# Turning the normed rows of the FFN stage by a round trip through memory and one VectorE instruction, in place of TensorE's transposes

## What is computed

```python
x   = x + tanh(g_xattn[0]) * xattn(_layernorm(x), ctx)          # stages 1 and 2
u   = _layernorm(x)                                             # stage 3 from here
mu  = mean(u); var = mean(square(u - mu))
h   = (u - mu) * rsqrt(var + EPS) * ln_gamma + ln_beta          # 4096 x 512
y   = silu(h @ w1 + fc1_bias)                                   # 4096 x 2048
z   = y @ w2 + fc2_bias                                         # 4096 x 512
out = x + tanh(g_ffn[0]) * (u + 0.5 * z)
```

## Time and profile before

| | us |
|---|---|
| median of 3 runs (1665.62 to 1668.49) | 1667.76 |
| the profiled execution | 1669.8 |
| its span in the trace | 1668.0 |
| PE busy in the span | 1631.2 |
| DVE busy | 848.6 |
| ACT busy | 569.1 |
| POOL busy | 366.3 |

### The profile page before, as it was taken

How to read it: one execution, slowest core, us unless ns; L and a number is a source line. 1 busy time by engine, 2 the same in 40 slices (tenths; PEclk the granted TensorE clock), 3 DMA queues, 4 the chain that set the end, 5 groups by cost and what they waited for, 6 DMA issues and landing times.

```text
span 1668.0 us, 20697 instructions
## 1 busy us (share of the span) xinstructions
PE 1631.2 (98%) x7746; PEld 1341.2 (80%) x7746; DVE 848.6 (51%) x1732; ACT 569.1 (34%) x990; POOL 366.3 (22%) x562
## 2 busy tenths in 40 slices
PE   8999999999999999899999899999999999999999
PEld 6887888877788887687877688888888888888887
DVE  6757454486764444688888955232333232333311
ACT  5432121234222112575666433232223222322322
POOL 1212100022111000488888801000000000000000
PEclk9999999999999999899999999999999999999999
DMA  6302110131221105454554432101010101010000
GB/s 210 107 21 95 44 51 26 49 109 52 70 76 39 38 26 170 133 164 152 164 165 158 132 109 74 40 1 51 1 51 1 51 1 51 1 51 1 26 1 26
DMA packets 66760, 116.19 MB, mean 70 GB/s; under 512 B 11185, under 2 KB 11185, under 8 KB 66507
## 3 DMA queue, kind: packets, MB, share of 16 engines
q1 hardware_dynamic: 64864, 111.41, 20.7%
q10 hardware_dynamic: 1797, 3.46, 0.6%
HBM read 80.00 MB, written 34.84 MB: 69 GB/s over the span
## 4 chain that ended last, share of the span: by engine, by line
PE 91%; DVE 4%; POOL 2%; issue 1%; DMA 1%; ACT 1%; DVEq 0%; SPq 0%; ACTq 0%; POOLq 0%
PE banks L719 86%; PE banks L729 3%; PE banks L929 2%; DVE split L1662 1%; DMA tile_x<-x_scratch 1%; DMA plain<-in_L_xattn_Wk 0%; POOL split L1537 0%; DVE plain L1793 0%; DVE split_q L1662 0%; DVE plain L2025 0%; POOL split L1544 0%; POOL small L1525 0%; ACT plain L1246 0%; DVE plain L2203 0%; DVE plain L2208 0%
## 5 line engine op out<-in xcount | busy, mean ns | idle before, releaser
L719 PE MATMUL banks<-split_q,split 128*128 128x512 f32 x2328 | 571.4, 395 | 4.9 <-POOL split L1537 3.2
L719 PE MATMUL banks<-split 128*128 128x512 f32 (+5 forms) x2304 | 543.4, 385 | 8.4 <-DVE split L1662 5.8
L719 PEld LDWEIGHTS banks<-split_q,split 128*128 128x128 f32 x2328 | 431.3, 188 | 96.2 <-POOL split L1537 4.1
L719 PEld LDWEIGHTS banks<-split 128*128 128x128 f32 (+3 forms) x2304 | 412.7, 185 | 106.7 <-DVE plain L1793 7.1
L719 PE MATMUL banks<-split,split_q 128*128 128x512 f32 (+3 forms) x1728 | 391.7, 379 | 7.2 <-DVE split_q L1662 4.3
L719 PEld LDWEIGHTS banks<-split,split_q 128*128 128x128 f32 x1728 | 308.3, 189 | 58.0 <-DVE split_q L1662 5.1
L1662 DVE TENSOR_TENSOR split<-banks,split 128x512 fp32r<-128x512 f32 (+5 forms) x232 | 146.3, 638 | 153.0 <-ACT split L1119 152.2
L2168 DVE TENSOR_TENSOR split<-plain,split 128x512 fp32r<-128x512 f32 x128 | 88.5, 692 | 257.8 <-ACT split L1438 257.8
L1119 ACT ACTIVATE split<-banks 128x512 fp32r<-128x512 f32 (+5 forms) x232 | 124.3, 557 | 247.2 <-PE banks L929 191.1
L1432 ACT ACTIVATE plain<-banks,small 128x512 f32<-128x512 f32 x128 | 88.0, 688 | 289.2 <-PE banks L719 289.2
L1662 DVE TENSOR_TENSOR split_q<-banks,split_q 128x512 fp32r<-128x512 f32 x68 | 46.7, 687 | 220.2 <-ACT split_q L1119 220.0
(11 more groups left out here) (155 smaller groups left out, 1259.2 us busy)
## 6 DMA issues: line engine op xcount, KB each, us to landing
plain<-in_x SPq DMA_DIRECT2D x64, 256.0 KB, 2.7
xo_scratch<-plain SPq DMA_DIRECT2D x32, 256.0 KB, 2.3
x_scratch<-plain SPq DMA_DIRECT2D x32, 256.0 KB, 2.0
plain<-x_scratch SPq DMA_DIRECT2D x32, 256.0 KB, 3.0
tile_x<-xo_scratch SPq DMA_DIRECT2D x32, 256.0 KB, 3.1
xg_scratch<-tile_x SPq DMA_DIRECT2D x32, 256.0 KB, 2.0
out<-plain SPq DMA_DIRECT2D x32, 256.0 KB, 2.1
tile_x<-x_scratch SPq DMA_DIRECT2D x28, 256.0 KB, 5.0
```

What stands on the lines that cost most here:

```text
L719: mm = nc.tensor.matmul(out, left(c, l), right(c, r), start=start and c == 0 and (l, r) == PASSES[0], stop=stop and c == chunks - 1 and (l ...
```

## The change

The next tile's normed block is no longer transposed by PE. SP stores the 128x512 block from `H0[:, 0]` to a scratch tensor in DRAM and reads it back with four loads into `HB` (the other half of `H0`). Load i fills partitions 32i to 32i+31; in them, each partition takes 16 runs of 32 floats (128 bytes). After that, the four loads together have placed every 32x32 square where its transpose belongs, but not yet turned in itself. One DVE instruction (`nc.vector.transpose`) turns all squares of the block in place, from `HB` into PSUM bank 2 or 3. `hi_h` and `lo_h` read the bank as before. Scaling and shifting are done one pass earlier (`NORM_AT = (6, 8, 10, 12)`), as are `base_x`, the statistics and the addition of `bias3`. `TURN_AT` is unchanged. `h_scale` waits for the store of the block before it, since the store reads the single buffer.

```diff
+NORM_AT = (6, 8, 10, 12)
 TURN_AT = (7, 9, 11, 13)
+QB = P // 32
...
+        h_dram = nc.dram_tensor("h_scratch", (TILE, E), F32, kind="Internal").ap()
...
+        HB = H0[:, 1]
...
+            def store_h(t, k):
+                sp.wait_ge(hn_ready, t * BT + k + 1)
+                if t > 1:
+                    sp.wait_ge(tp_full, (t - 1) * BT + TP3 + k + 1)
+                sp.dma_start(h_dram[k * P:(k + 1) * P, :], H0[:, 0]).then_inc(h_out, 16)
+            def load_hb(t, k):
+                sp.wait_ge(h_out, ((t - 1) * BT + k + 1) * 16)
+                sp.wait_ge(tp_full, t * BT + TP3 + k)
+                rows = h_dram[k * P:(k + 1) * P, :].rearrange("(q s) (c i r) -> i s c q r", q=QB, c=C, i=QB)
+                for i in range(QB):
+                    sp.dma_start(HB[32 * i:32 * i + 32].rearrange("p (c q r) -> p c q r", c=C, q=QB),
+                                 rows[i]).then_inc(hb_in, 16)
             for f in range(4, NF):
...
+                if f >= 8 and f % 2 == 0:
+                    store_h(1, f // 2 - 4)
+                    load_hb(1, f // 2 - 4)
...
             for t in range(NT):
+                if 0 < t < NT - 1:
+                    for k in range(BT):
+                        store_h(t + 1, k)
+                        load_hb(t + 1, k)
                 store_out(t, t % 2)
...
 # PE, tile3
                     ffn_out(t, f)
-                    if f in TURN_AT and not last:
-                        turn_h(t + 1, TURN_AT.index(f))
...
 # ACT, tile3
                     if f in TURN_AT and not last:
                         hi_h(t + 1, 1 - slot, TURN_AT.index(f))
-                    if f + 1 in TURN_AT and not last:
-                        k = TURN_AT.index(f + 1)
+                    if f + 1 in NORM_AT and not last:
+                        k = NORM_AT.index(f + 1)
                         base_x(t + 1, 1 - slot, k, base[:, 1 - slot, k])
...
 # DVE
             def h_scale(t, k, x):
-                dve.wait_ge(tp_full, t * BT + TP3 + max(k - 1, 0))
+                if t == 0:
+                    dve.wait_ge(tp_full, TP3 + max(k - 1, 0))
+                else:
+                    dve.wait_ge(tp_full, TP3 + BT)
+                    if (t - 1) * BT + k:
+                        dve.wait_ge(h_out, ((t - 1) * BT + k) * 16)
...
+            def turn_h(t, k):
+                dve.wait_ge(hb_in, ((t - 1) * BT + k + 1) * QB * 16)
+                nc.vector.transpose(PS[:, 2 + k % 2], HB).then_inc(tp_full, 1)
...
 # DVE, tile3, behind lo_hid3 (and, in tile 0, lo_w and scale_w2)
-                        if f + 2 in TURN_AT:
-                            k = TURN_AT.index(f + 2)
+                        if f + 2 in NORM_AT:
+                            k = NORM_AT.index(f + 2)
...
-                        if f + 1 in TURN_AT:
-                            h_shift(t + 1, TURN_AT.index(f + 1))
-                        if f - 1 in TURN_AT:
-                            k = TURN_AT.index(f - 1)
+                        if f + 1 in NORM_AT:
+                            h_shift(t + 1, NORM_AT.index(f + 1))
+                        if f in TURN_AT:
+                            turn_h(t + 1, TURN_AT.index(f))
+                        if f - 1 in NORM_AT:
+                            k = NORM_AT.index(f - 1)
...
-                        if f == TURN_AT[0] - 3:
+                        if f == NORM_AT[0] - 3:
                             stats_x3(p3, base[:, 1 - slot], (b_in[1 - slot], (t + 1) // 2 * 16 + 16 * (1 - slot)))
                         if f in TURN_AT:
                             lo_h(t + 1, 1 - slot, TURN_AT.index(f))
```

More of the change, by code:

```diff
@@ L428, in build @@
         o_out = [sem("o_out_0"), sem("o_out_1")]
+        h_out, hb_in = sem("h_out"), sem("hb_in")
         block = ctx.enter_context(nc.Block())
@@ L2200, in h_scale @@
             def h_scale(t, k, x):
-                dve.wait_ge(tp_full, t * BT + TP3 + max(k - 1, 0))
-                nc.vector.scalar_tensor_tensor(out=H0[:, k % 2], in0=x, scalar=mvX[:, k, 0:1], in1=vec3[:, 0],
+                if t == 0:
[4 more added lines that the diff above has]
+                        dve.wait_ge(h_out, ((t - 1) * BT + k) * 16)
+                nc.vector.scalar_tensor_tensor(out=H0[:, 0 if t else k % 2], in0=x, scalar=mvX[:, k, 0:1], in1=vec3[:, 0],
                                                op0=ALU.subtract, op1=ALU.mult).then_inc(x3_scaled, 1)
@@ L2207, in h_shift @@
                 dve.wait_ge(x3_scaled, t * BT + k + 1)
-                nc.vector.scalar_tensor_tensor(out=H0[:, k % 2], in0=H0[:, k % 2], scalar=rsH[:, k:k + 1],
+                h = H0[:, 0 if t else k % 2]
+                nc.vector.scalar_tensor_tensor(out=h, in0=h, scalar=rsH[:, k:k + 1],
                                                in1=vec3[:, 1], op0=ALU.mult, op1=ALU.add).then_inc(hn_ready, 1)
             def lo_h(t, slot, k):
-                lo_t(TP3 + k, [hT[:, slot * C:(slot + 1) * C, h, k * P:(k + 1) * P] for h in range(2)],
-                     k, t, BT)
+                halves = [hT[:, slot * C:(slot + 1) * C, h, k * P:(k + 1) * P] for h in range(2)]
+                lo(TP3 + k, halves[1], quarters(PS[:, 2 + k % 2]), halves[0], t, BT)
+            def turn_h(t, k):
+                dve.wait_ge(hb_in, ((t - 1) * BT + k + 1) * QB * 16)
+                nc.vector.transpose(PS[:, 2 + k % 2], HB).then_inc(tp_full, 1)
             kept = None
```

## The result

| | before | after |
|---|---|---|
| median, us | 1667.47 (4 runs) | 1653.12 (4 runs, 1652.21 to 1656.21) |
| profiled execution, us | 1669.8 | 1656.2 |
| its span, us | 1668.0 | 1654.4 |

The ratio is 0.9911, 95% interval 0.9897 to 0.9925. The kernel is 14.4 us faster; 19.2 were forecast. The direction and the range held, but 4.8 us are missing. The two traces say where.

A forecast was written before the change was run, and what follows sets the result against it. PE was taken as the bound, busy all of stage 3; removing 28 turns of 0.684 us saves 19.2 us, everything added being hidden at cost 0, so 1667.76 becomes 1648.6 us; range 1645.5 to 1660.

The forecast's parts named there:

- A turn costs 0.684 us of PE: Stage 3, PE: each of 28 turns, transposes plus the wait behind them, costs 0.684 us; removing all saves 19.2 us.
- DVE's transpose at 0.69 us: DVE, one added transpose per block: 0.69 us, ends 0.5 and 3.0, hidden behind PE's matmuls at cost 0.
- The round trip in steady tiles hidden: SP and DMA, tiles 1 to 6: store lands after 2.0 us, gather 3.3 us before DVE asks; cost 0.
- the bounds: DMA engines: a 128-byte packet takes near 0.018 us, with ends of 0.012 and 0.103 us.
- The cover of 3.4 us: DVE's transpose in a turn pass: it may come 3.4 us later than +3.94 and still cost PE nothing.
- Earlier statistics in tile 0: Tile 0, DVE: statistics moved earlier wait 1.1 us for the load of tile 1's rows, inside 2.94 us slack.
- SP's queue in tile 0: Tile 0: w2's loads queue behind `load_hb` by some 1 to 2 us; cost 0, up to 4 us kept for range.
- the next pass makes it up: Tile 0, DVE's turn passes: work plus wait exceeds 5.44 by 1.9 us, inside 2.94, and is recovered one pass later.
- rival B: Transposes go but a wait of the present size stays each turn, giving back 9.2 us: 1657.9; chance 0.09.
- Rival A: DVE's wait on `hb_in`: gather loads land too late, 65 us lost at the upper end, 1733 us; chance 0.08.
- Rival C: Gather loads split into 4-byte pieces, 4096 packets per engine, 1120 us more, near 2770; chance 0.02.
- the 100 of the estimate: Gather loads: by the Trainium skill's rule on plain DMAs that transpose by strides, a block would take some 100 us.

The follow-up runs named there:

- serial_4s: Changed kernel; in tiles 1 to 6 each gather load waits for the one before, and the block is stored three times in sequence: 1714.45 us, ratio 1.0274.
- serial_4: Changed kernel; in tiles 1 to 6 each gather load is issued when the one before has landed: 1653.14 us, ratio 0.991.
- no_trip_0: Changed kernel without tile 0's block stores and gather loads, so DVE turns what the buffer holds: 1648.03 us, ratio 0.9875.
- w2_and_base_first: Changed kernel with w2's odd load ahead of the gather and the load of tile 1's rows one pass earlier: 1649.42 us, ratio 0.9886.

## Why the prediction was right, and which term was wrong

- **A turn costs 0.684 us of PE** and all of it goes: right. Tiles 1 to 6 went from 89.78 to 87.04 us. The split of that cost was off: transposes 0.48 and wait 0.20, not 0.56 and 0.12. The sum did not hang on it, since both went.
- **DVE's transpose at 0.69 us**: 0.72 measured, inside the ends of 0.5 and 3.0.
- **The round trip in steady tiles hidden**: right, with the store landing after 2.0 us as taken. Each load's issue took 0.63 us, not 0.44. The packets cost less. The first window goes from a store to behind its gather, the other two split it into store and gather (columns as in the earlier trace rows):

```profile
1071.50:1080.00 8.50, 8.50 (x39) 7.05 (x38) 1.58 (x3) 1.46 (x3) 0.00 (x0) 1.00 0.28 62
...
1071.75:1073.80 2.05, 2.05 (x11) 1.70 (x10) 0.00 (x0) 0.00 (x0) 0.00 (x0) 1.00 0.34 128
1073.80:1078.20 4.40, 4.40 (x21) 3.66 (x20) 1.35 (x2) 1.32 (x2) 0.00 (x0) 1.00 0.38 60
```

  0.28 x 8.5 x 16 = 38 us of engine time. The store's 128 full packets took 0.34 x 2.05 x 16 = 11.2 of it, 0.087 us each, and the gather 0.38 x 4.4 x 16 = 26.8; over 2048 that is 0.013 us for a packet of 128 bytes, near the low end of the bounds. Taken with 0.087 for a full packet, the 4-byte pieces of the earlier trace rows come to (25.6 - 11.2) / 1024 = 0.014; the forecast's 0.012 was their least. The block landed 4.3 us before its use; 3.3 had been forecast.
- **The cover of 3.4 us**: right; 3.6 in serial_4s, and serial_4's waits of up to 2.1 us were free.
- **Earlier statistics in tile 0**: their wait was 2.8 us, not 1.1. The forecast took the median of 5.4 us for the load of tile 1's rows; this one lands after 7.3 us, and after 6.8 in the trace of before too. The wait cost nothing by itself, as no_trip_0 and w2_and_base_first show, but it left DVE and w2's loads late where the round trip begins.
- **SP's queue in tile 0: this is the term that failed.** The forecast put it at 0, with up to 4 us kept for the range; it cost 5.2 by PE's idle times. Three sizes were off. The store in tile 0 took 3.6 to 3.9 us, not 2.0, probably since w2's two loads were issued just before it (no run takes them away); the four issues took 2.6, not 1.8; and the odd unit's load was issued 4.3 us later than before the change (990.26, against 985.16 in a trace whose stage 3 begins 0.8 us earlier), not 1 to 2. Of these 4.3 us the round trip made 2.6: without it, in no_trip_0, the same load is 1.7 us late (984.19, in a trace whose stage 3 begins 2.6 us earlier than that of before), behind the statistics' wait. And a step of the reasoning was missing: "the next pass makes it up" holds for work that is late once. Here the late scaling holds back SP's next even load, with the next store behind it. The added wait sat in a loop of 12 us that must go round in 10.88. The 5.2 us are also more than the 4 that had been kept for this; the range held because it was made wide enough to take in rival B as well, and that is partly luck.
- **Rival A** (loads too late) came true nowhere, and its place was sought at the wrong queue item: not the gather was late but the load behind it. serial_4s made A true and gave its price. **Rival B** (one wait of 0.3 us each turn) did not occur; the total lay between it and the forecast for another reason. **Rival C**: per block 2048 small packets were moved, not 65536; the page counts 70769 packets under 512 bytes, 59584 more than before: 57344 for 28 blocks, and a rest of 2240, which is 28 x 5 DMAs x 16 engines (serial_4s, with 48 stores more, has 768 = 48 x 16 more). The rule of the Trainium skill (VectorE: DVE Perf Modes, section "The three transpose paths") about plain DMAs that transpose by strides is tied there to a large innermost stride on the destination's side. The gather of 128-byte runs is not that case: the four loads of a block land within 4.4 us of the first issue, not after the 100 of the estimate.

## What to carry to other kernels

A step moved to DMA must be checked against everything behind it in the issuing queue: add up the waits and issues of one round of that queue, together with the engines it feeds, and compare the sum with the time of the passes it serves. If a wait for a store must stand in a queue, put the next needed load between the store and that wait. And a layout change split into a gather of runs of 32 floats (no other length was run) and one VectorE transpose of 32x32 squares took a transposition off a busy TensorE at no cost, where the block could be some 10 us under way and the other engines had room.

## What had not been expected

A packet of 128 bytes took the engines about as long as one of 4 bytes, 0.013 us against 0.012 to 0.014. The issue of a gather load cost SP 0.63 us with 512 pieces, against 0.33 to 0.43 for loads and stores with 128. The number of pieces alone doesn't explain it: the load of a tile's rows has 512 pieces of 2 KB and takes 0.38, and the loads small<-x_scratch with 512 pieces take 0.37 and 0.51. What does was not tried. A store of the same size took 2.0 us in a quiet queue and 3.6 to 3.9 us right behind two loads of 256 KB. And in serial_4s PE came back at the 1.2 GHz level behind an idle time of 3.05 us (but stayed at full clock behind one of 2.97 at 1199.83), so a late operand cost more than its lateness.
